# Top-2 mixture stage: router tiles as half-array products, and the output sum split over ScalarE and GpSimd

## The chip, the cores and the metric

The kernel runs on one NeuronCore of a Trainium2 chip. The metric is the device time of one execution in microseconds, given as the median of several. Below, an "engine" is one of the core's instruction streams: TensorE (PE, with its weight loads PEld), VectorE (DVE), ScalarE (ACT), GpSimd (POOL) and SyncE (SP), which issues most DMAs here.

## The reference, cut to what matters

The whole program is a two-layer network on an input of 4 x 64 x 128 x 128 float32 (65,536 tokens of 64 channels). Only its last stage is touched:

```python
t = _to_tokens(x)
t = t + _L1_ffn_ref(_ln_t(t), router_w, router_b, expert_w, expert_b)

def _L1_ffn_ref(x, router_w, router_b, expert_w, expert_b):
    router_probs = softmax(x @ router_w + router_b)      # 8 experts
    top_p, top_i = top_k(router_probs, 2)
    top_p = top_p / sum(top_p)
    expert_out = einsum('bnd,edc->bnec', x, expert_w) + expert_b
    gathered = take_along_axis(expert_out, top_i[..., None], axis=2)
    return einsum('bnk,bnkc->bnc', top_p, gathered)
```

The kernel computes all eight experts for each token, with a gate of zero for those that weren't chosen: the token is multiplied by its gate first (a product called Z), and the sum over experts is gathered in PSUM. The stage's output is that sum plus the residual x.

## The kernel before, in words

The program runs in stages: a wavelet mixer, an expert choice, four scan passes, and from about 1660 us on the top-2 mixture (`top2_mixture`), which alone is changed.

**Tiling.** The tokens come in 64 chunks of 512 columns by 128 partitions (64 channels of two halves of a row, so 1024 tokens a chunk). Two chunks make a pair; slot i = 0 or 1 is the chunk's place in it. A pair moves through a software pipeline of 37 steps written out in Python, `for t in range(STEPS)` on each engine. In one step t PE does the router products of pair t (`tiles`), the gate transposes and the broadcasts of pair t-2 (`near`), and the experts of pair t-3 (`ex`).

**PE.** A step has four blocks, p = 0 to 3. Each block holds, in this order: `tiles` (one PSUM bank of router products; bank A for p = 0 and 2, bank B for p = 1 and 3), in blocks 0 and 2 the two parts of `biases`, two `broadcast` calls (a gate row spread over 64 partitions for each of the expert pair's halves, into `pg`), in blocks 0 and 2 `turn_gates` (four transposes), and two `experts` calls. An `experts` call is a product on each half of the array's columns: output partitions 0 to 63 and 64 to 127 of the bank `po[i]`. There are eight q per step (four expert pairs for each slot), so block p issues `broadcast` q = 2p+2 and 2p+3 and `experts` q = 2p and 2p+1. A float32 product is issued as two passes, so the trace counts two matmuls for each.

**VectorE.** For each q it forms Z(q) = pg x nd (`z_of`, L1685), where nd is a copy of the tokens. Between the Z it runs the top-2 search, whose pieces `choose(t, n)` are set by hand at certain q: pieces 9 and 10 (sum and reciprocal of the chosen weights of pair t-2) at q = 0, piece 0 of pair t-1 at q = 1, pieces 1 to 4 at q = 3, 5 at q = 5, 6 to 8 at q = 7. The output sum `y_of` (L1692, PSUM bank `po` plus the residual view of X, written to `yo`) stands at q = 1 (slot 1 of the pair before) and q = 5 (slot 0).

**ScalarE** reads the router banks (`read_tiles`: four squares with their sums and a copy for each bank), copies the turned gates from bank B to SBUF (`copy_gates`), and does the exponentials. **GpSimd** does, in each step: `weigh(t-2)`, `scale(t-1)`, `split(t-2)`, `lower`, the residual-stream sum `x3(t+1, 0)`, `lower` again, `x3(t+1, 1)`. **SyncE** loads x2, copies tokens to nd, and stores y.

Each engine works through its own list in order. The waits that matter below:

```python
# PE                                     # VectorE, choose(t, 9)
wait(pe, s["z"], t * UNITS + q - 1)      dve.wait_ge(s["weighed"], t + 1)
```

so the broadcast of q needs Z(q-2), since `pg` has two buffers, and piece 9 needs GpSimd's `weigh` of the same pair. `experts` of q needs Z(q).

Of the kernel before, what the change touches and what calls it, by code (L numbers as in the profile page):

```python
# [26 lines left out]
ACT = mybir.ActivationFunctionType  # L27
ALU = mybir.AluOpType
# [32 lines left out]
def wait(engine, sem, count):  # L61

    if not isinstance(count, int) or count > 0:
        engine.wait_ge(sem, count)
# [1323 lines left out]
def top2_mixture(nc, g, a, y_out):  # L1388
# [14 lines left out]
    with ExitStack() as ctx:  # L1403
# [20 lines left out]
        s = {n: m.sem(n) for n in (  # L1424
            "x3", "tiledA", "tiledB", "readA", "readB", "lnv", "rstd", "logits",
            "logits_used", "scaled", "shifted", "lowered", "exp", "chosen", "weighed", "inverse", "gates",
            "turned", "gcopied", "bcast", "z", "zmm", "y")}
        chain, pool_chain, act_chain = (m.sem(n) for n in ("chain", "pchain", "achain"))
        Xv = g.X[:].rearrange("p (s n) -> p s n", s=2)
        x_dst = y_out.rearrange("b c (j t) w -> b t c j w", t=2)  # L1430
# [2 lines left out]
        def xview(t, i):  # L1433

            k, u = divmod(t, 2)
            at = (2 * u + i) * HP * WP + k * (JR * WP)
            return Xv[:, :, at:at + JR * WP]

        def natural(t):

            return t.rearrange("p (j w v) -> p v j w", j=JR, v=2)
# [7 lines left out]
        def now(t):  # L1449

            return 0 <= t < PAIRS

        with nc.Block() as block:
# [39 lines left out]
            @block.tensor  # L1493
            def _(pe):
                def tiles(t, i, part):

                    n = 2 * t + i
                    wait(pe, s["x3"], n + 1)
                    bank, t0, done, free = order[part]
                    wait(pe, s[free], n)  # L1500
                    if bank is bankB:
                        wait(pe, s["gcopied"], n - 4)
                    for v in range(2):
                        last = pe.matmul(bank[:, v * TW:v * TW + TW], xview(t, i)[:, t0 // 2, v * P:v * P + P], rx[:],  # L1504
                                         start=True, stop=True)
                    last.then_inc(s[done], 1)

                def turn_gates(t, i, read):
                    wait(pe, s["gates"], t + 1)
                    wait(pe, s["gcopied"], 2 * t + i)  # L1510
                    wait(pe, s["readB"], min(read, CHUNKS))
                    for v in range(TILES):
                        last = pe.transpose(bankB[0:C, v * P:v * P + P],  # L1513
                                            gp[t % 2][:, i * TILES + v].rearrange("p a l e -> p (a l e)").bitcast(F32),
                                            unit[:])
                    last.then_inc(s["turned"], 1)

                def broadcast(t, q):
                    i, ep = divmod(q, EP)
                    if ep == 0:  # L1520
                        wait(pe, s["gcopied"], 2 * t + i + 1)
                    wait(pe, s["z"], t * UNITS + q - 1)
                    for h in range(2):
                        at, rows = h * E1 + 2 * ep, slice(h * C, h * C + 2 * G2)
                        last = pe.matmul(pg[q % 2][:, h * N:h * N + N], sel[rows, at:at + 2].rearrange("p e c -> p (e c)"),  # L1525
                                         gT[i][rows], start=True, stop=True)
                    last.then_inc(s["bcast"], 1)

                def biases(t, i, part):
                    if part == 0:  # L1530
                        wait(pe, s["y"], 2 * t + i - 1)
                    pe.matmul(po[i][:], bias[PLAIN, part], gT[i][PLAIN], start=(part == 0), stop=False,  # L1532
                              skip_group_check=True)

                def experts(t, q):
                    i, ep = divmod(q, EP)
                    wait(pe, s["z"], t * UNITS + q + 1)
                    for h in range(2):
                        last = pe.matmul(po[i][h * C:h * C + C, :], wexp[:, ep], Z[q % 4][:, h],  # L1539
                                         start=False, stop=(ep == EP - 1), skip_group_check=True)  # L1540
                    last.then_inc(s["zmm"], 1)

                for t in range(STEPS):
                    near, ex = t - 2, t - 3
                    for p in range(EP):
                        if now(t):
                            tiles(t, p // 2, p % 2)
                        for q in (2 * p + 2, 2 * p + 3):
                            if now(ex) and p % 2 == 0:
                                biases(ex, p // 2, q % 2)  # L1550
                            if q < UNITS and now(ex):
                                broadcast(ex, q)
                            if q >= UNITS and now(near):
                                broadcast(near, q - UNITS)
                        if now(ex) and p == 0:
                            turn_gates(ex, 1, 2 * t)
                        if now(near) and p == 2:
                            turn_gates(near, 0, 2 * t + 1)
                        if now(ex):
                            experts(ex, 2 * p)  # L1560
                            experts(ex, 2 * p + 1)

            @block.scalar
            def _(act):
# [29 lines left out]
                def copy_gates(t, i):  # L1594
# [3 lines left out]
                    act.activation(gT[i][0:C], bankB[0:C, :], ACT.Copy)  # L1598
                    act.activation(gT[i][C:C + 2 * G2], bankB[0:2 * G2, :], ACT.Copy).then_inc(s["gcopied"], 1)

                for t in range(STEPS):
                    near, ex = t - 2, t - 3
                    if now(ex):
                        copy_gates(ex, 1)
                    if now(t - 1):
                        wait(act, s["shifted"], t)
                        act.activation(EX[:], L[:], ACT.Exp).then_inc(s["exp"], 1)
                    if now(t):
                        read_tiles(t, 0)
                    if now(near):  # L1610
                        copy_gates(near, 0)
                    if now(t):
                        read_tiles(t, 1)
                        rstd(t)

            @block.gpsimd
            def _(pool):
                def x3(t, i):
                    wait(pool, x2_in[t % 2][i], (t // 2) * 16 + 16)
                    xv = xview(t, i).rearrange("p v (j w) -> p v j w", j=JR)  # L1620
                    pool.tensor_tensor(xv, natural(x2[t % 2][i][:]), xv, ALU.add).then_inc(s["x3"], 1)  # L1621

                def scale(t):
                    wait(pool, s["rstd"], t + 1)
# [33 lines left out]
                x3(0, 0)  # L1658
                x3(0, 1)
                for t in range(STEPS):  # L1660
                    if now(t - 2):
                        weigh(t - 2)
                    if now(t - 1):
                        scale(t - 1)
                    if now(t - 2):
                        split(t - 2)
                    if now(t - 1):
                        lower(t - 1, 1, "shifted")
                        pool.wait_ge(chain, (t - 1) * LINKS + 5)
                    if now(t + 1):  # L1670
                        x3(t + 1, 0)
                    if now(t - 1):
                        lower(t - 1, 6, "lowered")
                    if now(t + 1):
                        x3(t + 1, 1)

            @block.vector
            def _(dve):
                def z_of(t, q):
# [3 lines left out]
                    if ep == 0:  # L1683
                        wait(dve, nd_in[t % 2][i], (t // 2 + 1) * ND_SEM)
                    dve.tensor_tensor(Z[q % 4][:], pg[q % 2][:].rearrange("p (h n) -> p h n", h=2), nd[t % 2][i][:],  # L1685
                                      ALU.mult).then_inc(s["z"], 1)

                def y_of(t, i):
                    n = 2 * t + i
                    wait(dve, s["zmm"], (n + 1) * EP)  # L1690
                    wait(dve, y_st[i], t * 32)
                    dve.tensor_tensor(natural(yo[i][:]), po[i][:].rearrange("p (v j w) -> p v j w", v=2, j=JR),  # L1692
                                      xview(t, i).rearrange("p v (j w) -> p v j w", j=JR), ALU.add
                                      ).then_inc(s["y"], 1)

                def choose(t, n):

# [44 lines left out]
                for t in range(STEPS):  # L1742
                    for q in range(UNITS):
                        if now(t - 3):
                            z_of(t - 3, q)
                        if now(t - 2) and q == 0:
                            choose(t - 2, 9)
                            choose(t - 2, 10)
                        if now(t - 4) and q == 1:
                            y_of(t - 4, 1)  # L1750
                        if now(t - 1):
                            for n in {1: (0,), 3: (1, 2, 3, 4), 5: (5,), 7: (6, 7, 8)}.get(q, ()):
                                choose(t - 1, n)
                        if now(t - 3) and q == 5:
                            y_of(t - 3, 0)


class Shared:
# [91 lines left out]
```

## Time and profile before

| what | value |
|---|---|
| median of 3 runs | 2137.81 us (2135.49 to 2139.49) |
| span of the profiled execution, first to last instruction | 2135.2 us |
| PE busy in the span | 2023.2 us, 95% |
| VectorE busy | 1193.0 us, 56% |
| ScalarE busy | 1005.2 us, 47% |
| GpSimd busy | 511.6 us, 24% |
| mean granted TensorE clock | 0.969 of 2.4 GHz |

The profiled execution has no time of its own beside its span in these data; the span is 2.6 us below the median and 0.3 us below the fastest run. The page cuts the span into 40 slices of 53 us: the mixture is the last nine of them. Busy shares of PE count a matmul from its start to its modelled end, so back-to-back products overlap and a full PE reads 100%.

### The profile page before, as it was taken

How to read it: one execution, taken by the hardware profiler on the slowest of the kernel's cores; microseconds unless marked ns; L12 is line 12 of the kernel's file. 1: busy time of each engine (PE TensorE's matmuls, PEld its weight loads, DVE VectorE, ACT ScalarE, POOL GpSimd, SP SyncE). 2: the span in 40 equal slices, each digit the busy share in tenths (PEclk: the TensorE clock that was granted, in tenths of full speed). 3: DMA queues.
4: the chain of work that ended last, by engine and by line, in shares of the span. 5: the costliest groups of instructions: out<-in, count | busy, mean ns of one | idle time of the engine just before them, and what ended most of it. 6: DMA issues, size and time to landing. Idle time of an engine off the chain costs nothing. (4 is left out here: it accounts for less than half of the span.)

```text
span 2135.2 us, 40582 instructions
## 1 busy us (share of the span) xinstructions
PE 2023.2 (95%) x14414; PEld 1528.4 (72%) x14414; DVE 1193.0 (56%) x2548; ACT 1005.2 (47%) x2815; POOL 511.6 (24%) x622
## 2 busy tenths in 40 slices
PE   6999992699999989999999999999999799999998
PEld 3555551377777779999999999999999444444443
DVE  5777778666666653222222222232222599999998
ACT  4666664334444423333344444444444545455452
POOL 4555543222222210000000000000000554555541
PEclk9999996599999999999999999999999799999999
DMA  4955541223223210000000000000000466655653
GB/s 117 242 164 169 163 144 50 68 87 99 90 90 99 86 36 1 0 0 0 0 4 0 0 0 0 20 0 0 0 0 0 114 153 149 153 151 149 153 137 90
DMA packets 192672, 159.04 MB, mean 74 GB/s; under 512 B 25848, under 2 KB 159000, under 8 KB 192536
## 3 DMA queue, kind: packets, MB, share of 16 engines
q1 hardware_dynamic: 190840, 156.89, 26.4%
q8 instruction: 61, 1.00, 0.2%
q0 software_dynamic: 512, 0.53, 0.1%
q14 instruction: 75, 0.61, 0.1%
q10 hardware_dynamic: 1184, 0.00, 0.0%
HBM read 56.70 MB, written 67.11 MB: 58 GB/s over the span
## 5 line engine op out<-in xcount | busy, mean ns | idle before, releaser
L1208 PE MATMUL s_ps<-g_ring,g_T 128*128 128x128 f32 x7620 | 855.7, 274 | 8.5 <-DVE g_ring L1255 8.5
L1208 PEld LDWEIGHTS s_ps<-g_ring,g_T 128*128 128x128 f32 x7620 | 854.6, 192 | 9.2 <-DVE g_ring L1255 9.1
L1244 DVE SCALAR_TENSOR_TENSOR g_ring<-s_ps,s_xs 128x128 f32<-128x128 f32 x508 | 148.7, 293 | 418.3 <-PE s_ps L1208 418.3
L1685 DVE TENSOR_TENSOR tm_Z<-tm_pg,tm_nd 128x1024 f32<-128x1024 f32 x256 | 301.9, 1211 | 22.9 <-PE tm_pg L1525 22.5
L1307 ACT ACTIVATE g_X<-g_ring 128x256 f32<-128x256 f32 x254 | 172.3, 678 | 296.0 <-DVE g_ring L1244 296.0
L1539 PE MATMUL tm_po<-tm_Z,g_wexp 128*64 128x512 f32 x1024 | 249.2, 608 | 0.0
L1291 ACT ACTIVATE g_X<-g_ring 64x256 f32 x256 | 106.9, 418 | 205.5 <-DVE g_ring L1244 203.3
L1244 DVE SCALAR_TENSOR_TENSOR g_ring<-s_ps,g_X 128x128 f32<-128x128 f32 x254 | 74.4, 293 | 210.6 <-PE s_ps L1208 210.6
L1621 POOL TENSOR_TENSOR g_X<-g_x,g_X 128x512 f32<-128x512 f32 x64 | 82.9, 1298 | 349.7 <-POOLq L1184 286.0
L1302 ACT ACTIVATE s_xs<-g_X 128x256 f32<-128x256 f32 x254 | 161.3, 636 | 0.6 <-PEq L1184 0.6
L1539 PEld LDWEIGHTS tm_po<-tm_Z,g_wexp 128*64 128x64 f32 x1024 | 62.5, 137 | 109.9 <-issue 108.1
L1330 POOL MEMSET g_zero<- 128x1 f32 x1 | 0.1, 98 | 578.2 <-POOLq L1184 578.2
L1598 ACT ACTIVATE tm_gT<-tm_bankB 64x512 fp32r<-64x512 f32 x64 | 37.8, 591 | 202.0 <-PE tm_bankB L1513 202.0
L1004 PEld LDWEIGHTS af_ps<-g_yh,g_Tlo 128*128 128x128 f32 x635 | 85.0, 190 | 66.8 <-DVE g_yh L1115 54.3
L533 POOL TENSOR_TENSOR wm_sql<-g_X,wm_sqh 128x512 fp32r<-128x512 f32 x64 | 89.1, 1393 | 132.9 <-DVE wm_sqh L568 131.6
L1004 PE MATMUL af_ps<-g_yh,g_Tlo 128*128 128x256 f32 x635 | 111.5, 306 | 5.9 <-DVE g_yh L1115 4.2
L1115 DVE SCALAR_TENSOR_TENSOR g_yh<-af_ps,g_X 128x256 fp32r<-128x256 f32 x127 | 54.1, 426 | 90.4 <-PE af_ps L1008 87.7
L1008 PE MATMUL af_ps<-g_yl,g_Thi 128*128 128x256 f32 x635 | 99.2, 288 | 0.0
L1004 PE MATMUL af_ps<-g_yh,g_Thi 128*128 128x256 f32 x635 | 98.0, 285 | 0.0
L1525 PE MATMUL tm_pg<-tm_gT,g_sel 32*128 32x512 f32 x512 | 96.2, 449 | 1.2 <-DVE tm_Z L1685 1.1
L1008 PEld LDWEIGHTS af_ps<-g_yl,g_Thi 128*128 128x128 f32 x635 | 86.6, 192 | 0.0
L1004 PEld LDWEIGHTS af_ps<-g_yh,g_Thi 128*128 128x128 f32 x635 | 86.1, 190 | 0.0
(273 smaller groups left out, 2887.7 us busy)
## 6 DMA issues: line engine op xcount, KB each, us to landing
tm_nd<-g_X SPq DMA_DIRECT2D x256, 128.0 KB, 2.4
g_X<-in_x SPq DMA_DIRECT2D x128, 128.0 KB, 2.9
x1s<-g_X SPq DMA_DIRECT2D x64, 256.0 KB, 2.1
x1tok<-g_X SPq DMA_DIRECT2D x64, 256.0 KB, 2.5
g_x<-x2s SPq DMA_DIRECT2D x64, 256.0 KB, 2.9
y<-tm_yo SPq DMA_DIRECT2D x128, 128.0 KB, 2.5
g_X<-x1s SPq DMA_DIRECT2D x32, 256.0 KB, 2.8
x2s<-g_X SPq DMA_DIRECT2D x32, 256.0 KB, 2.0
```

The costliest lines, as they stand in the source:

```text
L533: pool.tensor_tensor(sq_lo[:], sq[c % 2], sq_hi[:].bitcast(F32), ALU.subtract).then_inc(s["parts"], 1)
L1004: pe.matmul(out, t[:, d * P:d * P + P], g.yh[:, :, d:d + 64], start=(t is g.Tlo and d == 0), stop=False)
L1008: last = pe.matmul(out, g.Thi[:, d * P:d * P + P], g.yl[:, :, d:d + 64], start=False, stop=(d == ND - 1))
L1208: last = pe.matmul(out, g.T[i][:, d * P:d * P + P], g.ring[(u - 1) % RING][:, images(c), d:d + 64], start=(d == 0), stop=(d == ND - 1))
L1244: dve.scalar_tensor_tensor(g.ring[n % RING][:, images(c), inner], conv, 0.0, x[:, images(c)], ALU.max, ALU.add).then_inc(y_ready[c], 1)
L1291: last = act.activation(dst.rearrange("p b j w -> p b (j w)"), src, ACT.Copy)
L1302: act.activation(xs[n % RING][:], line(*place(n)), ACT.Copy).then_inc(staged, 1)
L1307: act.activation(line(*place(n)), g.ring[n % RING][:, :, inner], ACT.Copy).then_inc(stored, 1)
L1525: last = pe.matmul(pg[q % 2][:, h * N:h * N + N], sel[rows, at:at + 2].rearrange("p e c -> p (e c)"), gT[i][rows], start=True, stop=True)
L1539: last = pe.matmul(po[i][h * C:h * C + C, :], wexp[:, ep], Z[q % 4][:, h], start=False, stop=(ep == EP - 1), skip_group_check=True)
L1621: pool.tensor_tensor(xv, natural(x2[t % 2][i][:]), xv, ALU.add).then_inc(s["x3"], 1)
L1685: dve.tensor_tensor(Z[q % 4][:], pg[q % 2][:].rearrange("p (h n) -> p h n", h=2), nd[t % 2][i][:], ALU.mult).then_inc(s["z"], 1)
```

## The change

Three things change in the mixture. (1) `tiles` issues each router product as two, one for each half of the array's columns (64 tokens of weights each, output on partitions 0 to 63 and 64 to 127), where it was one of 128 columns. (2) The output sum leaves VectorE: `y_of` is gone; ScalarE copies the bank `po[i]` to `yo[i]` (`evict`), and GpSimd adds the residual to `yo[i]` in place (`add_residual`). (3) The first bias product into `po[i]` waits for `evict`, not for the sum. The positions in each list are chosen by hand.

```diff
                     for v in range(2):
-                        last = pe.matmul(bank[:, v * TW:v * TW + TW], xview(t, i)[:, t0 // 2, v * P:v * P + P], rx[:],
-                                         start=True, stop=True)
+                        for h in range(2):
+                            at = v * P + h * C
+                            last = pe.matmul(bank[h * C:h * C + C, v * TW:v * TW + TW],
+                                             xview(t, i)[:, t0 // 2, at:at + C], rx[:], start=True, stop=True)
...
                 def biases(t, i, part):
                     if part == 0:
-                        wait(pe, s["y"], 2 * t + i - 1)
+                        wait(pe, s["evicted"], 2 * t + i - 1)
...
+                def evict(t, i):
+                    wait(act, s["zmm"], (2 * t + i + 1) * EP)
+                    wait(act, y_st[i], t * 32)
+                    act.activation(natural(yo[i][:]), po[i][:].rearrange("p (v j w) -> p v j w", v=2, j=JR), ACT.Copy
+                                   ).then_inc(s["evicted"], 1)
+
                 for t in range(STEPS):
                     near, ex = t - 2, t - 3
+                    if now(t - 4):
+                        evict(t - 4, 1)
                     if now(ex):
                         copy_gates(ex, 1)
...
                         read_tiles(t, 0)
+                    if now(ex):
+                        evict(ex, 0)
                     if now(near):
                         copy_gates(near, 0)
...
+                def add_residual(t, i):
+                    wait(pool, s["evicted"], 2 * t + i + 1)
+                    pool.tensor_tensor(natural(yo[i][:]), natural(yo[i][:]),
+                                       xview(t, i).rearrange("p v (j w) -> p v j w", j=JR), ALU.add
+                                       ).then_inc(s["y"], 1)
...
                 for t in range(STEPS):
+                    if now(t - 4):
+                        add_residual(t - 4, 1)
                     if now(t - 2):
                         weigh(t - 2)
...
                         lower(t - 1, 1, "shifted")
+                    if now(t - 3):
+                        add_residual(t - 3, 0)
+                    if now(t - 1):
                         pool.wait_ge(chain, (t - 1) * LINKS + 5)
                     if now(t + 1):
                         x3(t + 1, 0)
...
-                        if now(t - 4) and q == 1:
-                            y_of(t - 4, 1)
...
-                        if now(t - 3) and q == 5:
-                            y_of(t - 3, 0)
```

How the lists look at the places that matter:

GpSimd before, one step from its first instruction (L1639 and L1641 are `weigh`, L1626 and L1628 `scale`, L1652 to L1655 `split`, L1634 `lower`, L1621 `x3`):

```order
L1639 TENSOR_TENSOR tm_F<-tm_F 128x128 [waits tm_chosen]
L1641 TENSOR_TENSOR tm_F<-tm_F,tm_EX 128x128 [waits tm_exp,tm_pchain]
L1626 TENSOR_TENSOR tm_L<-tm_L,tm_R 128x128 [waits tm_logits,tm_rstd]
L1628 TENSOR_TENSOR tm_L<-tm_L,g_rbias 128x128 [waits tm_logits_used]
L1652 TENSOR_TENSOR tm_GG<-tm_F,tm_total 128x128 [waits tm_turned,tm_inverse]
L1653 TENSOR_TENSOR tm_GG<-tm_GG,tm_R 128x128 [waits tm_pchain]
L1654 TENSOR_TENSOR tm_gp<-tm_GG,g_zero 128x16x16 [waits tm_pchain]
L1655 TENSOR_TENSOR tm_gp<-tm_GG,tm_gp 128x16x16 [waits tm_pchain]
L1634 TENSOR_TENSOR tm_L<-tm_L,tm_m 128x128 [waits tm_chain]
L1621 TENSOR_TENSOR g_X<-g_x_00,g_X 128x2x256 [waits g_x2i00,tm_chain]
```

GpSimd with the change, the same step (L1637 is `add_residual`, L1657 and L1659 are now `weigh`, L1633 is `x3`):

```order
L1637 TENSOR_TENSOR tm_yo<-tm_yo,g_X 128x2x256 [waits tm_evicted]
L1657 TENSOR_TENSOR tm_F<-tm_F 128x128 [waits tm_chosen]
L1659 TENSOR_TENSOR tm_F<-tm_F,tm_EX 128x128 [waits tm_exp,tm_pchain]
L1644 TENSOR_TENSOR tm_L<-tm_L,tm_R 128x128 [waits tm_logits,tm_rstd]
L1646 TENSOR_TENSOR tm_L<-tm_L,g_rbias 128x128 [waits tm_logits_used]
L1670 TENSOR_TENSOR tm_GG<-tm_F,tm_total 128x128 [waits tm_turned,tm_inverse]
L1671 TENSOR_TENSOR tm_GG<-tm_GG,tm_R 128x128 [waits tm_pchain]
L1672 TENSOR_TENSOR tm_gp<-tm_GG,g_zero 128x16x16 [waits tm_pchain]
L1673 TENSOR_TENSOR tm_gp<-tm_GG,tm_gp 128x16x16 [waits tm_pchain]
L1652 TENSOR_TENSOR tm_L<-tm_L,tm_m 128x128 [waits tm_chain]
L1637 TENSOR_TENSOR tm_yo<-tm_yo,g_X 128x2x256 [waits tm_evicted]
L1633 TENSOR_TENSOR g_X<-g_x_00,g_X 128x2x256 [waits g_x2i00,tm_chain]
```

What moved: an instruction that waits for the eviction stands ahead of `weigh`, and a second one ahead of `x3`.

VectorE with the change, at the end of one step and the start of the next (L1708 is `z_of`, L1752 and L1755 are pieces 9 and 10, L1723 piece 0):

```order
L1749 TENSOR_TENSOR tm_F<-tm_A,tm_m 128x128 [waits tm_chain]
L1708 TENSOR_TENSOR tm_Z<-tm_pg,tm_nd 128x1024 [waits tm_nd00,tm_zmm,tm_bcast]
L1752 TENSOR_REDUCE tm_total<-tm_F 128x16 [waits tm_weighed]
L1755 RECIPROCAL tm_total<-tm_total 128x16 [waits tm_chain]
L1708 TENSOR_TENSOR tm_Z<-tm_pg,tm_nd 128x1024 [waits tm_zmm,tm_bcast]
L1723 TENSOR_REDUCE tm_m<-tm_L 128x16 [waits tm_scaled]
```

What moved: only the output sum is gone, which stood between the last two rows; piece 9 still stands ahead of Z(1).

## Rows read from the trace of the kernel before

**Rows 1.** The page: busy time of each engine, and PE's slices with the clock

```profile
PE 2023.2 (95%) x14414; PEld 1528.4 (72%) x14414; DVE 1193.0 (56%) x2548; ACT 1005.2 (47%) x2815; POOL 511.6 (24%) x622
...
PE   6999992699999989999999999999999799999998
```

**Rows 2.** Busy us (and instructions) by stretch; then granted clock, DMA share, GB/s

```profile
core 0: us, PE busy (x) PEld busy (x) DVE busy (x) ACT busy (x) POOL busy (x), PEclk, DMA share, GB/s
1085.60:1089.00 3.40, 3.40 (x16) 3.40 (x17) 0.49 (x2) 1.43 (x3) 0.00 (x0) 0.50 0.17 37
1373.90:1377.30 3.40, 3.40 (x31) 3.40 (x32) 0.58 (x2) 1.03 (x3) 0.00 (x0) 1.00 0.83 285
1662.50:1693.00 30.50, 21.15 (x70) 13.91 (x70) 14.15 (x31) 16.92 (x124) 18.32 (x30) 0.50 0.47 131
1700.00:2080.00 380.00, 380.00 (x2068) 165.21 (x2066) 354.33 (x572) 194.35 (x1180) 195.83 (x326) 1.00 0.60 150
```

**Rows 3.** PE's timeline, one step: start us, us, line, names, shapes, count

```profile
1855.67 1.94 PE L1539 MATMUL tm_po<-tm_Z,g_wexp 128*64 128x512 f32 x8
1857.53 0.76 PE L1504 MATMUL tm_bankA<-g_rx,g_X 128*128 128x144 f32 x4
...
1858.56 0.39 PE L1532 MATMUL tm_po<-tm_gT,g_bias 32*128 32x512 f32 x1
1858.56 0.39 PE L1525 MATMUL tm_pg<-tm_gT,g_sel 32*128 32x512 f32 x2
1858.88 0.63 PE L1513 MATMUL tm_bankB<-g_unit,tm_gp 128*64 128x128 f32 x4
...
1871.51 0.76 PE L1504 MATMUL tm_bankA<-g_rx,g_X 128*128 128x144 f32 x4
```

**Rows 4.** PE's timeline, short windows where experts end and router tiles begin

```profile
1850.00 0.60 PE L1539 MATMUL tm_po<-tm_Z,g_wexp 128*64 128x512 f32 x2
1850.53 0.51 PE L1504 MATMUL tm_bankA<-g_rx,g_X 128*128 128x144 f32 x2
...
1850.53 0.64 PE L1504 MATMUL tm_bankA<-g_rx,g_X 128*128 128x144 f32 x3
...
L1504 PE MATMUL tm_bankA<-g_rx,g_X x4: 286/286/390, 1850.5 to 1851.0; 128*128 128x144 f32 x4
```

**Rows 5.** VectorE's timeline around the start of a step

```profile
1855.55 1.23 DVE L1685 TENSOR_TENSOR tm_Z<-tm_pg,tm_nd 128x1024 f32<-128x1024 f32 x1 [0.58 <-PE tm_pg L1525]
1856.69 0.28 DVE L1737 TENSOR_REDUCE tm_total<-tm_F 128x16 f32<-128x128 f32 x1
1857.00 0.25 DVE L1740 RECIPROCAL tm_total<-tm_total 128x16 f32<-128x16 f32 x1
1857.17 1.16 DVE L1685 TENSOR_TENSOR tm_Z<-tm_pg,tm_nd 128x1024 f32<-128x1024 f32 x1
1858.25 0.68 DVE L1692 TENSOR_TENSOR tm_yo<-tm_po,g_X 128x512 f32<-128x512 f32 x1
```

**Rows 6.** GpSimd's timeline there (`weigh`), and groups by line of the mixture

```profile
1855.05 0.46 POOL L1639 TENSOR_TENSOR tm_F<-tm_F 128x128 f32<-128x128 f32 x1 [2.15 <-DVE tm_F L1734]
1855.58 0.46 POOL L1641 TENSOR_TENSOR tm_F<-tm_F,tm_EX 128x128 f32<-128x128 f32 x1
...
L1621 POOL TENSOR_TENSOR g_X<-g_x,g_X 128x512 f32<-128x512 f32 x64 | 82.9, 1298 | 349.7 <-POOLq L1184 286.0 <-DVE tm_L L1722 63.7
```

**Rows 7.** ScalarE, groups by line: copies of a PSUM bank and gates' copies

```profile
L485 ACT ACTIVATE g_X<-wm_xc 128x512 f32<-128x512 f32 x64 | 38.3, 598 | 71.3 <-PE wm_xc L411 71.3
L1598 ACT ACTIVATE tm_gT<-tm_bankB 64x512 fp32r<-64x512 f32 x64 | 37.8, 591 | 202.0 <-PE tm_bankB L1513 202.0
```

**Rows 8.** PE's timeline at three stops of the scan passes, idle time in brackets

```profile
794.35 1.96 PE L1208 MATMUL s_ps<-g_ring,g_T 128*128 128x128 f32 x12 [2.87 <-DVE g_ring L1255]
...
1085.60 3.77 PE L1208 MATMUL s_ps<-g_ring,g_T 128*128 128x128 f32 x17 [2.99 <-DVE g_ring L1255]
...
1373.75 0.94 PE L1208 MATMUL s_ps<-g_ring,g_T 128*128 128x128 f32 x6 [2.65 <-DVE g_ring L1255]
```

More of the change, by code:

```diff
@@ L1426, in top2_mixture @@
             "logits_used", "scaled", "shifted", "lowered", "exp", "chosen", "weighed", "inverse", "gates",
-            "turned", "gcopied", "bcast", "z", "zmm", "y")}
+            "turned", "gcopied", "bcast", "z", "zmm", "evicted", "y")}
         chain, pool_chain, act_chain = (m.sem(n) for n in ("chain", "pchain", "achain"))
@@ L1686, in z_of @@
                                       ALU.mult).then_inc(s["z"], 1)
[L1688 to L1694, printed above, removed]
                 def choose(t, n):
```

## The prediction

> **What bounds the kernel now.** I read the page's slices first: PE is at 9 tenths in the nine slices of the mixture, but for its first and last [rows 1]. Then the table by stretches, for the mixture's steady part, 1700 to 2080 us: PE 380.00 us of 380, clock 1.00, VectorE 354.33, GpSimd 195.83, ScalarE 194.35 [rows 2]. Two engines are near full there, so the question is which one waits for the other; PE's timeline says that. One step runs from the bank A tiles at 1857.53 to those at 1871.51, 13.98 us [rows 3], the same at each step I looked at, and PE starts its next group as the last one ends. PE bounds the steady part. It has little in hand on the other side, though: the second broadcast pair of block 0 starts at 1858.56 [rows 3], and the Z(1) that it needs ends at 1857.17 + 1.16 = 1858.33 [rows 5]. Whatever makes Z(1) late by more than 0.2 us stops PE.
>
> **Part 1, the router tiles.** What the rows show: two passes of `experts` on the two column halves start together at 1850.00, the tiles at 1850.53 [rows 4]. Two such pairs in the eight-pass group take (1857.53 - 1855.67) / 4 = 0.465 us on average [rows 3], and 512 columns stream in about 0.43, so 0.10 us of the 0.53 is a pause before the tiles. Then the second tile pass starts at 1850.53 + 0.51 - 0.286 = 1850.75, 0.22 after the first, while the third comes 0.13 later [rows 4]: 0.10 us more is the first weight load, which nothing covers. With the half-array form the tiles have the shape of `experts` ahead of them, so both should go: about 0.21 us for each `tiles` call. The eight half passes should take the time of the four whole ones, since halves started together in the experts rows. Bounds: nothing gained, if the pause stays and short passes don't pair (then even +0.5 us a call, four more passes of 0.12), and 0.21 gained; I take 0.21, because `experts` is nearest in form. Four calls a step: -0.83 us, if PE stays the bound. The Trainium skill, "TensorEngine Tiling (Array Packing)", Key Properties, says that changing the tiling mode drains TensorE; the 0.10 us before the tiles agrees.
>
> **Part 2, the output sum.** VectorE loses two sums of 0.68 us a step [rows 5]. Alone that gives nothing, as PE is the bound. ScalarE gains two bank copies; the nearest row is a 128x512 copy from PSUM, 598 ns [rows 7]. They fall where ScalarE is idle, waiting for the turned gates (202.0 us of idle before them in 64 cases, [rows 7]), so they cost nothing by themselves. The bias's wait moves to the eviction, a step earlier than needed: nothing. GpSimd gains two sums of the shape of `x3`, 1.298 us each [rows 6]: 2.6 us on top of 195.83 / 380 x 14.0 = 7.2 us a step [rows 2], so it is not full.
>
> Where they stand is what costs. The order of GpSimd's list puts `add_residual(t-4, 1)` first in the step, ahead of `weigh(t-2)`. It needs `evict(t-4, 1)`, which needs the last `experts` of the PE step before, and that ends at E = 1855.67 + 1.94 = 1857.61 [rows 3]. But `weigh` ran at 1855.05 [rows 6], 2.6 us before E. So `weigh` is pushed to behind E; VectorE's piece 9 waits for it with Z(1) queued behind; and the broadcast of q = 3, with everything after it on PE, waits for Z(1). The new path from E, each step from a row:
>
> - ScalarE's copy: 0.03 to notice + 0.60 [rows 7]
> - GpSimd's sum: 0.05 + 1.30 [rows 6]
> - `weigh`: 0.05 + 0.99 (1855.05 to 1855.58 + 0.46, [rows 6])
> - pieces 9 and 10: 0.05 + 0.48 (1856.69 to 1857.17, [rows 5])
> - Z(1): 1.20, and 0.05 until PE starts
>
> Together 4.80 us from E to the broadcast pair, where it was 1858.56 - 1857.61 = 0.95 [rows 3]. (The 0.03 to 0.05 hand-overs are estimates from the gaps between a releasing row's end and the released row's start.) From that pair to the next E it was 13.98 - 0.95 = 13.03; three of the four tile calls lie there, -0.62, and a weight load that is no longer covered, +0.1: 12.5. It closes a loop of one step: E releases the sum, the sum releases the rest of the step, and that ends in the next E. New step 4.80 + 12.5 = 17.3 us, +3.3. It needs a pair t-4 to finish and a pair t-2 to weigh: t = 4 to 33, 30 steps. 30 x 3.3 = **+99 us**. The other sum, `add_residual(t-3, 0)`, waits for the fourth expert pair and holds `x3(t+1, 0)` and `lower`; both have some 3 us in hand in a step made longer, and I cost it at nothing, at most its own 1.3 us a step. SyncE's store of y comes later too, with the token copies of pair t-1 behind it; their Z is more than a step away: nothing. After the last expert product a copy and a sum stand where one sum stood: 0.60 + 1.30 - 0.68 = +1.2 us once.
>
> **Part 3, the clock.** In each such step PE has nothing to start from the end of the first broadcast pair and the bias, about E + 1.15, to E + 4.8: a stop of 3.65 us. The trace has three stops of near that length at full clock: after 2.87 and 2.99 us of idle [rows 8] the next stretch ran at half the 2.4 GHz (0.50 at 1085.6 to 1089.0, [rows 2]); after 2.65 us at 1373.75 [rows 8] it didn't (1.00, [rows 2]). Ours is longer than all three, so I take it that the clock falls in every step. The price: 16 passes in 3.40 us where 31 ran in the same time at full clock [rows 2], 15 x 3.40 / 31 = 1.65 us for one such stretch. How soon it rises again is open: after the scan's stop, with full products, one stretch; in the start of the mixture it stayed at 0.50 for 30.5 us with PE busy 21.15 of them [rows 2], in the same mixed work of tiles, broadcasts and transposes. I take two stretches, less what lies in the stop itself: 3.0 us a step, 30 x 3.0 = **+90 us**. Bounds: nothing, and half clock for all PE work of the step, 12.5 us more.
>
> **Sum:** 2137.8 + 99 + 90 + 1 = 2328, less 1 us for tiles in the few steps outside the loop: **2327 us**. The sum is made on the profiled execution, whose span, 2135.2, is 2.6 us below the median; it is added to the median.
>
> **The Trainium skill against this change:** "SBUF — State Buffer" (the shared port pair) states that GpSimd and a VectorE instruction with two SBUF inputs lock each other out for a whole instruction. Z reads one of its inputs from PSUM, so by the rule the new sums pass beside it; only the search's pieces would be held, some 1.3 us a step for the sum of slot 0, and the sum of slot 1 runs while VectorE waits. No row here shows a piece that was held; by the page, if all of that came on the path, it would be 30 x 1.3 = 39 us more, which my range holds.
>
> **The rivals.**
> - *Clock stays up* (0.19). The stop is there, but it doesn't bring the clock down, as at 1373.75. 2137.8 + 99 + 1 - 1 = 2237, with 2228 to 2250 for hand-overs and the sum's length.
> - *The slot-1 sum is off the path* (0.07), faster: if GpSimd's sum is over before piece 9 is due at 1856.69, PE stays the bound, and each step loses 0.83 us: 32 x 0.83 = 27, 2112 us. It decides at Z(1): 0.2 us of lateness. Against it stands that the sum can't start before E, 0.9 us after 1856.69.
> - *Half clock nearly throughout* (0.12): the clock doesn't rise between stops, each step is 25 to 30 us: from 2440 up to 2137.8 + 30 x (3.3 + 12.5) = 2612.
> - *No change within the measurement* (0.02): gain of part 1 and a much smaller stop cancel.
> - The forecast, stop and one to three low stretches a step: 0.60; 2285 for one, 2385 for three, with the port lock 2420.
>
> The range from 2228 to 2425 takes in the forecast and the first rival. Times here agree to about 0.2% (4 us), so that is what can be told from no change: faster 0.07, same 0.02, slower 0.91.
>
> **What would show it.** In the profile after: steps of 17 to 21 us where they were 13.98; PE idle once a step, some 3.6 us, before L1527 and released by VectorE's Z; VectorE idle before piece 9, released by GpSimd's `weigh`; GpSimd idle before its sum, released by ScalarE; clock of 0.5 in part of each step; the next tile pass 0.43 after the last expert pair, no 0.22 between first and second. I am wrong if GpSimd's sum for slot 1 starts while PE still runs the experts that it needs, if PE's idle per step is under 2 us, or if the mixture's clock reads 1.00 throughout with a step over 18 us.

## The result, and the profile after

The changed kernel takes **2314.53 us** (median of 4, 2313.05 to 2318.41) where the kernel before takes 2136.65 in the same comparison: ratio 1.0837, 95% interval 1.0824 to 1.0850. It is slower by 178 us. The forecast was 2327 with a range from 2228 to 2425.

The page's first rows answer to [rows 1]; the last line below is PE's granted clock by slice:

```profile
PE 2094.3 (90%) x14926; PEld 1556.9 (67%) x14926; DVE 1190.2 (51%) x2484; ACT 1046.4 (45%) x2879; POOL 589.0 (25%) x686
...
PE   6999972899999899999999999999878888888887
...
PEclk9999995799999999999999999999878888888888
```

The mixture, last on the right, is no longer full, and its clock is at 8 tenths where it was at 9 or more. The stretches say how that comes about (length, then busy us and instruction counts of PE, PEld, VectorE, ScalarE and GpSimd, then granted clock, DMA share, GB/s):

```profile
1750.00:2250.00 500.00, 410.28 (x2306) 177.99 (x2306) 330.18 (x479) 210.06 (x1125) 242.16 (x354) 0.84 0.42 104
1968.60:1975.30 6.70, 6.27 (x22) 2.54 (x22) 3.90 (x8) 2.39 (x12) 2.11 (x4) 0.50 0.37 88
1975.50:1988.90 13.40, 10.16 (x70) 4.44 (x70) 9.33 (x12) 5.95 (x33) 7.58 (x11) 1.00 0.42 113
```

Before, PE had 380.00 us of 380 at clock 1.00 [rows 2]. Now it has 410.28 of 500 at 0.84, and one step splits into 6.7 us at half the 2.4 GHz and 13.4 us at full. Where PE stands still is in its timeline; this piece answers to [rows 3]:

```profile
1962.38 1.94 PE L1541 MATMUL tm_po<-tm_Z,g_wexp 128*64 128x512 f32 x8
1964.14 0.66 PE L1506 MATMUL tm_bankA<-g_rx,g_X 128*64 128x144 f32 x8
1964.73 0.49 PE L1534 MATMUL tm_po<-tm_gT,g_bias 32*128 32x512 f32 x1
...
1965.07 0.39 PE L1534 MATMUL tm_po<-tm_gT,g_bias 32*128 32x512 f32 x1
1969.03 0.80 PE L1527 MATMUL tm_pg<-tm_gT,g_sel 32*128 32x512 f32 x2 [3.57 <-DVE tm_Z L1708]
1969.76 1.06 PE L1515 MATMUL tm_bankB<-g_unit,tm_gp 128*64 128x128 f32 x4
1970.75 3.68 PE L1541 MATMUL tm_po<-tm_Z,g_wexp 128*64 128x512 f32 x8
```

PE is idle for 3.57 us (in the brackets) before the second broadcast pair (L1527), released by VectorE's Z, once in each step. The 1.94 us of the experts (L1541) before the stop are 3.68 after it: that is the low clock. Now the chain that leads to Z, on ScalarE (first row), GpSimd and VectorE (to set beside [rows 5, 6]):

```profile
1964.36 0.63 ACT L1606 ACTIVATE tm_yo<-tm_po 128x512 f32<-128x512 f32 x1 [0.79 <-PE tm_po L1541]
...
1965.07 1.29 POOL L1637 TENSOR_TENSOR tm_yo<-tm_yo,g_X 128x512 f32<-128x512 f32 x1 [2.43 <-ACT tm_yo L1606]
1966.31 0.45 POOL L1657 TENSOR_TENSOR tm_F<-tm_F 128x128 f32<-128x128 f32 x1
1966.84 0.45 POOL L1659 TENSOR_TENSOR tm_F<-tm_F,tm_EX 128x128 f32<-128x128 f32 x1
...
1967.33 0.28 DVE L1752 TENSOR_REDUCE tm_total<-tm_F 128x16 f32<-128x128 f32 x1 [2.76 <-POOL tm_F L1659]
1967.65 0.25 DVE L1755 RECIPROCAL tm_total<-tm_total 128x16 f32<-128x16 f32 x1
1967.82 1.16 DVE L1708 TENSOR_TENSOR tm_Z<-tm_pg,tm_nd 128x1024 f32<-128x1024 f32 x1
```

Each row starts within 0.1 us of the end of the one before it: last expert product (the prediction's E) 1964.32, copy 1964.36, sum 1965.07, `weigh` 1966.31, pieces 9 and 10 at 1967.33, Z(1) 1967.82 to 1968.98, PE 1969.03. From E to the broadcast it is 4.71 us, where it was 0.95 before. The steps (from one step's first bank A tiles to the next's) are 18.8 to 20.4 us, 19.92 on average, where they were 13.98.

### The profile page after: what moved, and what is told of

It reads as the page before. It is cut to its first block and busy times, and to the rows that moved or that the text cites. A ratio compares the mean times of both kernels' runs of the same rounds, so it can differ in the third digit from the quotient of the medians.

```text
span 2316.3 us, 41670 instructions
## 1 busy us (share of the span) xinstructions
PE 2094.3 (90%) x14926; PEld 1556.9 (67%) x14926; DVE 1190.2 (51%) x2484; ACT 1046.4 (45%) x2879; POOL 589.0 (25%) x686
## 5 line engine op out<-in xcount | busy, mean ns | idle before, releaser
L1708 DVE TENSOR_TENSOR tm_Z<-tm_pg,tm_nd 128x1024 f32<-128x1024 f32 x256 | 301.9, 1211 | 106.2 <-PE tm_pg L1527 106.0
L1541 PE MATMUL tm_po<-tm_Z,g_wexp 128*64 128x512 f32 x1024 | 296.4, 707 | 0.0
L1527 PE MATMUL tm_pg<-tm_gT,g_sel 32*128 32x512 f32 x512 | 114.4, 503 | 108.2 <-DVE tm_Z L1708 108.1
L1637 POOL TENSOR_TENSOR tm_yo<-tm_yo,g_X 128x512 f32<-128x512 f32 x64 | 82.7, 1293 | 320.0 <-ACT tm_yo L1606 320.0
L1541 PEld LDWEIGHTS tm_po<-tm_Z,g_wexp 128*64 128x64 f32 x1024 | 70.6, 155 | 135.8 <-issue 104.3
L1633 POOL TENSOR_TENSOR g_X<-g_x,g_X 128x512 f32<-128x512 f32 x64 | 82.9, 1297 | 290.5 <-POOLq L1184 287.5
L1527 PEld LDWEIGHTS tm_pg<-tm_gT,g_sel 32*128 32x128 f32 x512 | 45.7, 205 | 142.0 <-DVE tm_Z L1708 121.9
```

Source lines behind the costliest of these rows:

```text
L1637: pool.tensor_tensor(natural(yo[i][:]), natural(yo[i][:]), xview(t, i).rearrange("p v (j w) -> p v j w", j=JR), ALU.add).then_inc(s["y"], 1)
```

## The experiments

**1. The tiles alone.** The kernel before with the first hunk of the diff only; the sum stays on VectorE.

```diff
# kernel before
-                        last = pe.matmul(bank[:, v * TW:v * TW + TW], xview(t, i)[:, t0 // 2, v * P:v * P + P], rx[:],
+                        for h in range(2):
+                            at = v * P + h * C
+                            last = pe.matmul(bank[h * C:h * C + C, v * TW:v * TW + TW],
+                                             xview(t, i)[:, t0 // 2, at:at + C], rx[:], start=True, stop=True)
```

> The kernel before with the router tiles on the column halves; the output sum stays on VectorE. My theory (0.2 us saved at each of 128 tile calls as long as PE bounds the step): steps of 13.15 us, 2137 - 27 = 2110 us; VectorE was busy 13.0 us of each step, so if it becomes the bound a little less is saved, up to 2120 us. Rival (the half passes don't pair, or the pause before the tiles stays): 2137 us or above, with the first broadcast 0.69 us after the first tile pass as before.

Measured: 2118.51 us, ratio 0.9913 (0.9897 to 0.9930), 19 us faster. PE's timeline, and VectorE's Z(1):

```profile
1901.23 1.94 PE L1541 MATMUL tm_po<-tm_Z,g_wexp 128*64 128x512 f32 x8
1903.00 0.66 PE L1506 MATMUL tm_bankA<-g_rx,g_X 128*64 128x144 f32 x8
1903.59 0.49 PE L1534 MATMUL tm_po<-tm_gT,g_bias 32*128 32x512 f32 x1
...
1903.95 0.49 PE L1527 MATMUL tm_pg<-tm_gT,g_sel 32*128 32x512 f32 x2
1904.37 0.63 PE L1515 MATMUL tm_bankB<-g_unit,tm_gp 128*64 128x128 f32 x4
...
1902.73 1.16 DVE L1687 TENSOR_TENSOR tm_Z<-tm_pg,tm_nd 128x1024 f32<-128x1024 f32 x1
```

The row of the kernel before that belongs beside it, the first bias behind the tiles of [rows 3]:

```profile
1858.22 0.49 PE L1532 MATMUL tm_po<-tm_gT,g_bias 32*128 32x512 f32 x1
```

Experts to tiles takes 1.77 us where it took 1.86 ([rows 3], 1857.53 - 1855.67), tiles to the next product 0.59 where it took 0.69 (1857.53 to 1858.22): both pauses are gone and the half passes run in pairs, which saves 0.19 to 0.20 us a call. Four calls would be 0.8 us; the step is 13.35, 0.63 less than 13.98. Part of the rest is in the rows: the second broadcast pair starts at 1903.95, not with the second bias, and from it to the transposes it is 0.42 us where it was 0.32 ([rows 3], 1858.56 to 1858.88). Z(1) ends at 1902.73 + 1.16 = 1903.89, and the pair starts 0.06 us behind it, with 0.49 us on its row where it had 0.39: it comes later than PE could take it, so its weights are loaded in the open, 0.1 us a step. The expectation of 2110 missed by 8. The time lies in its second case, up to 2120, but that case blames VectorE's length, which experiment 9 doesn't bear out.

**2. The moved sum alone.** The changed kernel with whole tiles again (the hunk of experiment 1 taken back).

> The changed kernel with the router tiles whole again; only the output sum is moved to ScalarE and GpSimd. My theory (the slowdown is all from where GpSimd's sum stands): the loop from the last expert product through copy, sum, weigh, pieces 9 and 10 and Z(1) stays, PE stops some 3.5 us a step, and the three tile calls inside the loop cost 0.6 us more a step: about 2315 + 19 = 2334 us, 2315 to 2350 with the clock's phase. Rival (the half-array tiles cause part of the slowdown): below 2300 us.

Measured: 2330.46 us (two runs, 2328.55 and 2332.38), ratio 1.0904 (1.0882 to 1.0926), steps of 20.47 us on average. The tiles have no part in the slowdown; they give back about 16 us of it. The time is inside the expected 2315 to 2350.

**3. One call moved in GpSimd's list.** The changed kernel, `add_residual(t - 4, 1)` behind `split` and `lower`.

```diff
# changed kernel
-                    if now(t - 4):
-                        add_residual(t - 4, 1)
                     if now(t - 2):
                         weigh(t - 2)
...
                         lower(t - 1, 1, "shifted")
+                    if now(t - 4):
+                        add_residual(t - 4, 1)
                     if now(t - 3):
                         add_residual(t - 3, 0)
```

> The changed kernel with one call moved: GpSimd's sum for slot 1 stands behind split and lower, just ahead of the sum for slot 0; same instructions, same counts. My theory (order, not work): weigh runs before the last expert product ends again, no stop of PE before the broadcast of q = 3, clock 1.00 in the mixture, steps of 13.2 to 13.6 us, 2112 to 2125 us. Rival (the added work itself, GpSimd's 2.6 us and ScalarE's 1.3 us a step or the port that GpSimd shares with VectorE, costs the time): it stays above 2200 us.

Measured: 2149.70 us, ratio 1.0062 (1.0045 to 1.0080). The stop of 3.6 us is gone (one of about 0.7 us is left) and the mixture's clock is 1.00: the same instructions in another order are worth 165 us. But it isn't the 2112 to 2125 that was expected; steps are 14.49 us, and the kernel is 31 us slower than experiment 1. The groups of VectorE (mean ns behind the busy time) show one thing that I had priced at nothing; first this kernel, then experiment 1:

```profile
L1743 DVE SCALAR_TENSOR_TENSOR tm_A<-tm_L,g_rev 128x128 f32<-128x128 f32 x26 | 35.7, 1373 | 10.0 <-POOL tm_L L1652 10.0
L1726 DVE SCALAR_TENSOR_TENSOR tm_A<-tm_L,g_rev 128x128 f32<-128x128 f32 x26 | 24.7, 951 | 0.0
```

```profile
L1730 DVE SCALAR_TENSOR_TENSOR tm_A<-tm_L,g_rev 128x128 f32<-128x128 f32 x28 | 7.9, 281 | 0.0
L1713 DVE SCALAR_TENSOR_TENSOR tm_A<-tm_L,g_rev 128x128 f32<-128x128 f32 x28 | 7.8, 280 | 0.0
```

Pieces 6 and 1 of the search take 1373 and 951 ns where they take 281 and 280. Both read two operands from SBUF, and beside each runs a GpSimd sum of 1.3 us. That GpSimd's timeline of the same kernel shows for piece 6, which ran from 1914.58 for 1.37 us:

```profile
1911.63 1.29 POOL L1637 TENSOR_TENSOR tm_yo<-tm_yo,g_X 128x512 f32<-128x512 f32 x1 [3.55 <-ACT tm_yo L1606]
1912.88 1.30 POOL L1633 TENSOR_TENSOR g_X<-g_x,g_X 128x512 f32<-128x512 f32 x1
1914.13 0.41 POOL L1652 TENSOR_TENSOR tm_L<-tm_L,tm_m 128x128 f32<-128x128 f32 x1
1914.50 1.30 POOL L1633 TENSOR_TENSOR g_X<-g_x,g_X 128x512 f32<-128x512 f32 x1
```

The sum of slot 0 pushes `lower` (L1652) back until piece 6 waits for it, and the next GpSimd sum, `x3` of slot 1, starts just ahead of piece 6 and ends at 1915.80; piece 6 ends at 1915.95, 0.15 us behind it. How much of the 31 us is the late `lower` and how much the held pieces, this run doesn't say.

**4. The stop filled with PE work.** The changed kernel with idle products in the stop. They add zero to an output bank that is still being summed, so the result is the same and nothing is left out.

```diff
# changed kernel
                             if q < UNITS and now(ex):
+                                if q == 3 and ex > 0 and now(near):
+                                    for _ in range(14):
+                                        pe.matmul(po[0][:, 0:P], zero[:, 0:1].to_broadcast([P, P]), unit[:],
+                                                  start=False, stop=False, skip_group_check=True)
                                 broadcast(ex, q)
```

> The changed kernel, with 14 products of zero weights added into a column range of the open output bank on PE (they add zero) between the second bias product and the wait of the broadcast of q = 3, in 29 steps: some 3.2 us of PE work inside a stop of 3.6 us. My theory (of the 178 us, about 100 are the loop and 75 the clock that falls at each stop): the loop is as long as before, the clock stays at 1.00 in the mixture, steps of 17.2 us, 2235 to 2250 us. Rival (the clock is a bystander and the loop itself is 19.9 us long): 2300 us or above even with the clock up.

Measured: 2234.38 us (2233.97 and 2234.79), ratio 1.0454 (1.0433 to 1.0475): 80 us faster than the changed kernel by adding work to it. PE's timeline, then the stretch of 1750 to 2150 us:

```profile
1908.83 0.39 PE L1534 MATMUL tm_po<-tm_gT,g_bias 32*128 32x512 f32 x1
1909.15 3.39 PE L1556 MATMUL tm_po<-g_unit,g_zero 128*128 128x128 f32 x28
1912.80 0.49 PE L1527 MATMUL tm_pg<-tm_gT,g_sel 32*128 32x512 f32 x2 [0.26 <-DVE tm_Z L1712]
```

```profile
1750.00:2150.00 400.00, 394.06 (x2786) 217.74 (x2781) 304.83 (x441) 195.30 (x1049) 222.54 (x323) 1.00 0.49 124
```

The broadcast still waits for Z (0.26 us), so the loop is untouched, but the clock is 1.00 and every step is 17.25 us, as expected (17.2); the total is just under the expected 2235 to 2250. The loop costs 17.25 - 13.98 = 3.27 us a step, the clock 19.92 - 17.25 = 2.67.

**5. A wait without work.** The kernel before, and GpSimd waits for the last expert product ahead of `weigh`.

```diff
# kernel before
                 for t in range(STEPS):
+                    if now(t - 4):
+                        wait(pool, s["zmm"], (2 * (t - 4) + 2) * EP)
                     if now(t - 2):
                         weigh(t - 2)
```

> The kernel before with one wait added and no work: GpSimd waits, ahead of weigh, until the last expert product of the pair before is done (the semaphore that ScalarE's copy waits for in the changed kernel). My theory (the position of the wait makes the loop; the copy and the sum only lengthen it): from the last expert product to the second broadcast pair 0.05 + 0.99 + 0.05 + 0.48 + 1.20 + 0.05 = 2.8 us where it was 0.95, a step of 15.8 to 15.9 us, 30 x 1.87 = +56: 2193 us, 2188 to 2200, with PE idle some 1.6 us a step, too short for the clock to fall. If the clock falls too, 2240 to 2280. Rival (the copy and the sum themselves are what costs): 2137 to 2145 us.

Measured: 2243.11 us (2242.61 and 2243.61), ratio 1.0503 (1.0482 to 1.0524). The position alone costs 107 us, loop and clock together, with no work added to any engine. The number came out in the second case, 2240 to 2280 with the clock; the first, a stop too short for the clock to fall, failed: of 27 steps five are 15.94 us, just above the 15.8 to 15.9 of the loop, 19 are 17.5 to 17.6, and three 19.06. PE's timeline has a stop of 1.48 us in each, and in 22 of the 27 steps a part at half clock comes behind it; the stretches below show one such part and the 13.4 us after it:

```profile
1909.36 1.94 PE L1539 MATMUL tm_po<-tm_Z,g_wexp 128*64 128x512 f32 x8
...
1914.13 0.50 PE L1525 MATMUL tm_pg<-tm_gT,g_sel 32*128 32x512 f32 x2 [1.48 <-DVE tm_Z L1687]
...
1915.22 3.48 PE L1539 MATMUL tm_po<-tm_Z,g_wexp 128*64 128x512 f32 x8
```

```profile
1740.90:1744.30 3.40, 3.40 (x11) 0.81 (x9) 3.16 (x6) 2.39 (x12) 1.09 (x2) 0.50 0.33 77
1744.40:1757.80 13.40, 11.92 (x66) 5.24 (x64) 9.30 (x15) 4.73 (x31) 5.46 (x9) 1.00 0.55 138
```

From E (1909.36 + 1.94 = 1911.30) to the broadcast it is 2.83 us here, where it was 0.95 before and is 4.71 in the changed kernel. So of the 3.76 us that the changed kernel adds, one half is the position of the wait, and the other the copy and the sum that stand in it.

**6. The sum one place later.** The changed kernel, `add_residual(t - 4, 1)` between `weigh` and `scale`.

```diff
# changed kernel
-                    if now(t - 4):
-                        add_residual(t - 4, 1)
                     if now(t - 2):
                         weigh(t - 2)
+                    if now(t - 4):
+                        add_residual(t - 4, 1)
```

> The changed kernel with GpSimd's sum for slot 1 one place later, behind weigh and ahead of scale. My theory (loops through whatever is queued behind the sum): Z(1) is free, the step's wait moves to piece 0, split and pieces 1 to 4, which delay Z(2) and Z(4): steps of 14.5 to 15.5 us, 2150 to 2185 us, no low clock. Rival (any wait of GpSimd on the last expert product costs the whole loop): 2290 us or above.

Measured: 2180.61 us (2179.98 and 2181.25), ratio 1.0211 (1.0190 to 1.0231), steps of 15.38 us, clock 1.00, all as expected. The wait has moved, also as expected, to piece 0, which needs `scale`. VectorE's timeline:

```profile
1904.41 1.16 DVE L1708 TENSOR_TENSOR tm_Z<-tm_pg,tm_nd 128x1024 f32<-128x1024 f32 x1
1907.26 0.29 DVE L1723 TENSOR_REDUCE tm_m<-tm_L 128x16 f32<-128x128 f32 x1 [1.69 <-POOL tm_L L1646]
```

One place in a list is worth 134 us here, because the first thing behind the sum is due later.

**7. Whether GpSimd's sum holds the search's pieces.** Experiment 3 with one more wait: `x3` of slot 1 starts only when piece 6 is done.

```diff
# kernel of experiment 3
                         lower(t - 1, 6, "lowered")
+                        pool.wait_ge(chain, (t - 1) * LINKS + 7)
                     if now(t + 1):
                         x3(t + 1, 1)
```

> sum_behind_lower with one wait added: GpSimd's x3 of slot 1 waits until VectorE's piece 6 is done. In sum_behind_lower piece 6 (two SBUF inputs) took 1373 ns beside that x3, where it takes 281 in halves_only. Theory A (the two engines lock each other out of a shared SBUF port): piece 6 is back at about 281 ns, the step 0.7 to 1.1 us shorter, 2149.7 - 20 to 30 = 2120 to 2130 us. Theory B (piece 6 is slow for its position or its data, not for x3): it stays at 1.37 us and the time at 2150 us.

Measured: 2145.75 us, ratio 1.0051 (1.0034 to 1.0068), steps of 14.28 us. The duration came out as theory A says; the time didn't, as 2120 to 2130 was expected. VectorE's timeline (L1744 is piece 6, L1750 piece 8), then GpSimd's:

```profile
1913.64 0.29 DVE L1744 SCALAR_TENSOR_TENSOR tm_A<-tm_L,g_rev 128x128 f32<-128x128 f32 x1 [0.39 <-POOL tm_L L1652]
1913.97 0.29 DVE L1747 TENSOR_REDUCE tm_m<-tm_A 128x16 f32<-128x128 f32 x1
1914.29 1.17 DVE L1750 TENSOR_TENSOR tm_F<-tm_A,tm_m 128x128 f32<-128x128 f32 x1
...
1914.01 1.30 POOL L1633 TENSOR_TENSOR g_X<-g_x,g_X 128x512 f32<-128x512 f32 x1 [0.41 <-DVE tm_A L1744]
```

Piece 6 is back at 0.29 us, and piece 8, which also reads two operands from SBUF and took 0.29 in experiment 3, now takes 1.17: it ends at 1915.46, just behind the GpSimd sum at 1915.31. Piece 7 (L1747), with one operand, ran beside the start of that sum and took its usual 0.29. So it is the company, not the place of the piece, that makes it slow; the wait only changed which piece is held.

**8. Both sums where VectorE does Z.** The kernel of experiment 3 with slot 1's sum behind piece 4 and slot 0's at the end of the step.

```diff
# kernel of experiment 3
-                    if now(t - 4):
-                        add_residual(t - 4, 1)
-                    if now(t - 3):
-                        add_residual(t - 3, 0)
                     if now(t - 1):
                         pool.wait_ge(chain, (t - 1) * LINKS + 5)
+                    if now(t - 4):
+                        add_residual(t - 4, 1)
                     if now(t + 1):
                         x3(t + 1, 0)
...
                         x3(t + 1, 1)
+                    if now(t - 3):
+                        add_residual(t - 3, 0)
```

> The changed kernel with both of GpSimd's sums at places where VectorE does Z: slot 1's behind piece 4, ahead of x3 of slot 0, and slot 0's at the end of the step, behind x3 of slot 1. If only order and the port cost time, PE bounds the step again as in halves_only: 2115 to 2125 us, pieces 1 and 6 at 280 ns. If GpSimd's list is too long for these places, pieces 6 to 8 come late and weigh with them: 2130 to 2150 us.

Measured: 2118.63 us, ratio 0.9923 (0.9906 to 0.9939), steps of 13.30 us. VectorE's row for piece 6 with the GpSimd sum ahead of it, and the stretch of 1750 to 2080 us, in which PE has 329.88 us of 330 and bounds the step:

```profile
1910.64 0.40 DVE L1743 SCALAR_TENSOR_TENSOR tm_A<-tm_L,g_rev 128x128 f32<-128x128 f32 x1
1909.59 1.30 POOL L1637 TENSOR_TENSOR tm_yo<-tm_yo,g_X 128x512 f32<-128x512 f32 x1
```

```profile
1750.00:2080.00 330.00, 329.88 (x2269) 152.80 (x2266) 302.08 (x473) 207.94 (x1107) 238.22 (x345) 1.00 0.61 155
```

The same instructions as the changed kernel, 196 us faster, and PE is full again. Piece 6 meets only the end of a sum (1909.59 + 1.30 = 1910.89) and takes 0.40 us, not quite the 0.28 that was expected. Moving the sums is then worth nothing over experiment 1, as PE bounds both.

**9. One sum each.** Experiment 1 with only slot 1's sum on ScalarE and GpSimd, at the place of experiment 8 (`evict` in ScalarE's list, `add_residual` in GpSimd's, each for slot 1 alone and with semaphores of their own; the last hunk is VectorE's).

```diff
# kernel of experiment 1
+                    if now(t - 4):
+                        evict(t - 4)
...
                         pool.wait_ge(chain, (t - 1) * LINKS + 5)
+                    if now(t - 4):
+                        add_residual(t - 4)
...
-                        if now(t - 4) and q == 1:
-                            y_of(t - 4, 1)
```

> halves_only with only slot 1's sum moved: ScalarE copies the bank at the start of the step, GpSimd adds behind piece 4, ahead of x3 of slot 0; slot 0's sum stays on VectorE. If VectorE's full list is what holds halves_only at 13.35 us a step, it has 0.6 us less here and PE bounds at 13.2: 2137 - 31 x 0.78 = 2113 us, 2110 to 2117. If something else holds the 13.35 (the hand-over from Z to the broadcasts), it stays at 2118 us.

Measured: 2118.83 us (5 runs), ratio 0.9916 (0.9903 to 0.9930). VectorE had 10 us less to do in 330, and the time is that of experiment 1. Steps are 13.30 us, 0.05 less than there, and the second broadcast pair still starts behind the second bias, with 0.42 us to the transposes:

```profile
1903.56 0.39 PE L1534 MATMUL tm_po<-tm_gT,g_bias 32*128 32x512 f32 x1
1903.59 0.49 PE L1527 MATMUL tm_pg<-tm_gT,g_sel 32*128 32x512 f32 x2
1904.01 0.62 PE L1515 MATMUL tm_bankB<-g_unit,tm_gp 128*64 128x128 f32 x4
```

So VectorE's length is at most 0.05 us a step of what is left; the hand-over of Z(1) is 0.1 us of it. I didn't try to move Z(1) ahead of pieces 9 and 10. Nothing I ran is faster than experiments 1, 8 and 9, which can't be told apart.

## Why the prediction was right

- **PE bounded the steady part, with 0.2 us in hand at Z(1).** Right: experiment 5, which adds no work and makes the second broadcast pair 1.88 us later behind E, makes the steps in which the clock stays up 1.96 us longer.
- **Part 1, 0.21 us a tile call.** Measured 0.19 to 0.20 in experiment 1. The 0.83 us a step became 0.68 in experiments 8 and 9 and 0.63 in experiment 1: the four calls give 0.78, and 0.1 us of weight load came into the open in block 0. This sum left out that a PE which arrives earlier meets Z(1); the sum of part 2 has it, as +0.1. The last 0.05 of experiment 1 stays open.
- **Part 2, the loop.** The sum of its steps was 4.80 us from E to the broadcast, measured 4.71; the step 17.3, measured 17.25 with the clock held up. The terms: copy 0.60 against 0.63, sum 1.30 against 1.29, `weigh` 0.99 against 0.98, pieces 9 and 10 0.48 against 0.49, Z(1) 1.20 against 1.16 (its row in [rows 5] has 1.16 too, so 1.20 was 0.04 too much). 30 x 3.27 = 98 us against the 99 forecast, and experiment 4, which has the loop without the low clock, is 97 us above the 2137.33 of its own comparison.
- **Part 3, the clock.** It fell at each of the 30 stops, as forecast, but the ground for it was thin: I had ranked three stops of one profiled execution by length, and other executions don't bear that ranking out (last section). Two low stretches a step was a choice between one and three. That both came out so near is in part luck. I took 3.0 us a step; measured 2.67, or 80 us against 90: the low part lasted 3.4 us in five of the steps and 6.8 us in 25, and some of it lay in the stop, where it costs nothing. This is the term that makes 2327 of what was 2314.5. The first rival, clock stays up, fell; its price of 2237 was right, as experiment 4 shows (2234). The rival of half clock nearly throughout fell too: the clock rose again in every step, after 6.8 us at most, in the 30 steps. (Its lower end of 2440 doesn't follow from its steps of 25 us, 2137.8 + 30 x 11.0 = 2468.)
- **The other sum at nothing.** Right in the changed kernel, where the stop hides it: from the broadcast pair to the next E experiment 4 has 12.5 us, as forecast without it. Wrong once the stop is gone: experiment 3 is 31 us above experiment 1, with `lower` late and pieces 1 and 6 held. I had named the port as a rule and put at most 39 us on it. In my text no row showed a held piece; the changed kernel's rows show one (piece 6 at 1299 ns on average, the row at the end of this section), hidden by the stop. The Trainium skill, "SBUF — State Buffer", "SBUF: two separate sides", states that a GpSimd instruction that reads SBUF and a VectorE instruction with two SBUF inputs exclude each other for a whole instruction, and experiments 3 and 7 agree: 1.37 and 1.17 us where 0.29 is the piece alone. Z, with an input in PSUM, kept its 1211 ns.
- **The faster rival.** It needed GpSimd's sum to be out of the way of piece 9. The changed kernel isn't that, but experiments 8 and 9 are, and they give 17 to 19 us, not the 27 that I had worked out with 0.83 us a step (2137.8 - 27 is 2111, where I wrote 2112).
- **The signs.** All that the prediction named are in the rows: steps of 18.8 to 20.4 us, PE idle 3.57 us before L1527, piece 9 waiting for `weigh` (2.76), GpSimd's sum waiting for ScalarE (2.43), 0.5 of the clock in part of each step, and in the trace the tile pass 0.43 us behind the last expert pair. None of the signs of being wrong is.

```profile
L1743 DVE SCALAR_TENSOR_TENSOR tm_A<-tm_L,g_rev 128x128 f32<-128x128 f32 x30 | 39.0, 1299 | 10.8 <-POOL tm_L L1652 10.8
```

## What to carry to other kernels

Work moved to an idle engine can cost far more than its own length, through what stands behind it in that engine's list: ask when its input is ready, and who waits for the first instruction behind it. Its length then counts as well, since it lies in the same path (half of the delay here). Here the same instructions gave 2315, 2181, 2150 and 2119 us at four places. Where the engine that bounds the kernel feeds a stage that feeds it back, write the loop down from row to row and add it up; its sum was right to 0.1 us. And count the clock in: a stop of PE cost nearly as much again after it as the loop itself did.

## What the runs showed of the hardware that I had not expected

- A PE stop of only 1.48 us a step (experiment 5) was followed by half clock in 22 of 27 steps, while one of 2.65 us in the scan passes of the kernel before was not [rows 8]. The changed kernel has the same stop at the same place, and there the clock fell (its timeline, then its stretch). The profiles of all eleven kernels here have that stop, and the one of 2.99 us near 1085 us. Behind the 2.65 us the clock was at half in four (the changed kernel, experiments 2, 5 and 9); behind the 2.99 us it stayed full in four others (experiments 3, 4, 7 and 8). So which of equal stops lowers the clock is not set by its length alone; I didn't find out by what.

```profile
1374.78 1.44 PE L1208 MATMUL s_ps<-g_ring,g_T 128*128 128x128 f32 x5 [2.65 <-DVE g_ring L1255]
```

```profile
1374.70:1378.00 3.30, 3.22 (x15) 0.50 0.84 286
```

The trace of the kernel before already had a case against the length that the prediction didn't look at: a stop of 2.63 us ahead of the mixture (below), and after one more gap, of 0.74 us, half clock from 1662.4 us on.

```profile
1660.94 0.76 PE L1504 MATMUL tm_bankA<-g_rx,g_X 128*128 128x144 f32 x4 [2.63 <-POOL g_X L1621]
```

- The clock's price comes in lumps of 1.5 to 1.6 us: the steps of experiment 5 come in three lengths, 15.94, 17.55 and 19.06 us.
- Fourteen idle products a step, 3.39 us of PE, made the kernel 80 us faster by holding the clock.
- VectorE's 128x128 instruction with two SBUF inputs takes 1.37 us when a GpSimd sum of 1.30 us has just begun, against 0.28 alone.
